# Behind the scan: halves joined by a ScalarE copy and a VectorE sum, and one GpSimd sum for the mean over 192

## The chip, the cores and the metric

The kernel runs on one core of one Trainium2 chip. The metric is the device time of one launch in microseconds, for a batch of eight images. Engines are named as in the profile: PE is TensorE, DVE is VectorE, ACT is ScalarE, POOL is GpSimd (Pool in the text), SP is SyncE, which here only issues DMAs.

## The reference, cut to what matters

Each image is 96 channels of 64 x 64 pixels. Layer 0 is a visual state space block: group norm, layer norm, a projection to 192 channels, a depthwise convolution, a selective scan in four directions, the sum of the four, a layer norm over the 192 channels, a gate, a projection back to 96, and then a channel attention block. Layer 1 is linear attention and a quantised feed-forward part. The change lies where the scan's result is normalised:

```python
y = out_y[:, 0] + inv_y[:, 0] + wh_y + invwh_y          # four directions, 192 channels
y = jnp.transpose(y, (0, 2, 1)).reshape(b, H, W, D_INNER)
y = layer_norm(y, on_g, on_b)                           # mean and variance over 192
y = y * jax.nn.silu(z)
return jnp.einsum('bhwd,cd->bhwc', y, out_proj_w)
```

## The kernel before

Channels lie on partitions, the 4096 pixels of an image on the free axis. The 192 channels don't fit on 128 partitions. The first 128 are in `ya`. The last 64 (`DR`) are in `y5`, in two halves: partitions 0 to 63 hold the sum over two of the scan's directions, partitions 64 to 127 that over the other two, and the value of a channel is the sum of both halves. ACT writes the last of `y5` at the very end of the scan.

For each of the eight images, `prep_a`, `prep_b`, `scan` and `post` run one after the other, each as a block of its own with its own instruction list per engine; an engine starts a block when all have left the one before. Semaphores order the engines within a block.

`post` (line 1345) works in eight chunks j of 512 pixels (`CH`). The order of the work on each engine is written out with `staggered`: at step t an engine does the stages with the largest lag first, each for chunk t minus its lag. The stages that matter here are those of the layer norm over 192:

- PE, lag 0, `fold(j)` (L1383 to L1387): a product of `fold_w` (which adds partition p and p + 64) with `y5` gives the 64 joined channels in the PSUM bank `yr`; two products with `ones_di` (1/192 everywhere), of `ya` and of `y5`, add up to the mean in the bank `on_mean`. Behind them comes `var_192(j - 1)` (L1396), the mean of the squares of the chunk before, which waits for Pool (`sq_added`).
- ACT, lag 1, `ln_root` (L517, L519): Ln and Exp make the inverse deviation of chunk t - 1. Then, lag 0, `yr_copy` (L1544) copies the joined channels from PSUM to `yrc`, and `on_square` (L1548, L1549) squares both centred parts once DVE has centred them.
- DVE, lag 0, `on_center` (L1662, L1664): subtracts the mean from `ya` and, once the copy is there, from `yrc`. Ahead of it in a step DVE has, from the larger lags, `ln_unit` (L524), `skip2` (L1694), `ln_center` (L507), `skip` (L1688), `on_unit` (L1669, L1671) and `gate` (L1680, L1683).
- Pool (L1641): adds the squares of the 64 channels into those of the first 64 partitions, `sqa`. Behind the eighth it clears two rows of `cpad` (L1644, L1645), and PE's first convolution product `cab1(0)` (L1415), at step 8, waits for that.

Other products of PE in a step: `out_proj` (L1402, L1403), and the sums over 96 channels for the next layer norm (L502). An f32 product of 128 x 512 shows as two instructions in the trace, so a row with x2 is one product of the code.

SP issues the DMAs that bring the gates back at the start of the block, and then clears the semaphores of the stages before. DVE waits for them in `gate(0)` and `gate(2)`.

Of the kernel before, what the change touches and what calls it, by code (L numbers as in the profile page):

```python
# [17 lines left out]
F32 = mybir.dt.float32  # L18
# [3 lines left out]
ALU = mybir.AluOpType  # L22
# [7 lines left out]
DR = DI - DA  # L30
# [15 lines left out]
NCH = L // CH  # L46
# [67 lines left out]
def build(nc, x, weights, phase_weights, setup_weights, out, gate_dram, gn_dram):  # L114
# [8 lines left out]
    def put(name, shape, dt):  # L123

        size = int(np.prod(shape[1:])) * (4 if dt == F32 else 2 if dt in (BF16, F16) else 1)
        t = nc.alloc_sbuf_tensor_at(name, shape, dt, offset=place[0])
        place[0] += (size + 31) // 32 * 32
        return t
# [7 lines left out]
    fold_w = put("fold_w", [128, 128], F32)  # L136
# [16 lines left out]
    KB16 = L * 4  # L153
# [4 lines left out]
    def big(name, slot, parts=128):  # L158
        return at(name, [parts, L], F32, slot)
# [73 lines left out]
    yrc = big("yrc", 5 * KB16, DR)  # L233
    sqa = big("sqa", KB16)
# [40 lines left out]
    with ExitStack() as ctx:  # L275
# [11 lines left out]
        post_names = """x_nat_in x_tok_in gn_stats gn_dve mean_mm gn_mm gn_act scales_ready back_first back_in yr_mm  # L287
        yr_copied on_mean_mm on_centered on_squared on_var_mm on_log on_rsqrt on_unit sq_added gated
# [88 lines left out]
        with nc.Block() as block:  # L377
# [22 lines left out]
            def _(dve):  # L400
# [6 lines left out]
                low, up = col("ident")[:, 0:DR], col("ident")[:, DR:128]  # L407
                nc.vector.tensor_tensor(fold_w[:, 0:DR], low, up, ALU.add)
                nc.vector.tensor_tensor(fold_w[:, DR:128], low, up, ALU.add)

# [60 lines left out]
        def sl(j):  # L471

            return slice(j * CH, (j + 1) * CH)
# [871 lines left out]
        def post(img, b):  # L1345
            bank = dict(zip(("yr0", "on_mean0", "on_var", "out", "ln2_mean", "ln2_var", "yr1", "on_mean1"),
# [5 lines left out]
            with nc.Block() as block:  # L1352
# [25 lines left out]
                def _(pe):  # L1378

                    def fold(j):  # L1380

                        wait_free(pe, S["on_centered"], j, 2)
                        pe.matmul(bank[f"yr{j % 2}"], fold_w[:, :], y5[:, sl(j)], start=True, stop=True)\  # L1383
                          .then_inc(S["yr_mm"], 1)
                        mean = bank[f"on_mean{j % 2}"]
                        pe.matmul(mean, col("ones_di"), ya[:, sl(j)], start=True, stop=False)
                        pe.matmul(mean, col("ones_di"), y5[:, sl(j)], start=False, stop=True)\  # L1387
                          .then_inc(S["on_mean_mm"], 1)
                        if j > 0:
                            var_192(j - 1)  # L1390
# [94 lines left out]
                    staggered((0, fold), (1, lambda j: var_192(j) if j == NCH - 1 else None), (3, out_proj),  # L1485
# [53 lines left out]
                def _(act):  # L1539
                    ln_exp_tables(act)  # L1540

                    def yr_copy(j):
                        act.wait_ge(S["yr_mm"], j + 1)
                        act.copy(yrc[:, sl(j)], bank[f"yr{j % 2}"][0:DR, :]).then_inc(S["yr_copied"], 1)  # L1544
# [92 lines left out]
                def _(pool):  # L1637

                    for j in range(NCH):
                        pool.wait_ge(S["on_squared"], j + 1)  # L1640
                        pool.tensor_tensor(sqa[0:DR, sl(j)], sqa[0:DR, sl(j)], sqr[:, sl(j)], ALU.add)\  # L1641
                            .then_inc(S["sq_added"], 1)
# [16 lines left out]
                def _(dve):  # L1659
                    def on_center(j):  # L1660
                        dve.wait_ge(S["on_mean_mm"], j + 1)
                        dve.tensor_tensor(ya[:, sl(j)], ya[:, sl(j)], bank[f"on_mean{j % 2}"], ALU.subtract)  # L1662
                        dve.wait_ge(S["yr_copied"], j + 1)
                        dve.tensor_tensor(yrc[:, sl(j)], yrc[:, sl(j)], bank[f"on_mean{j % 2}"][0:DR, :], ALU.subtract)\  # L1664
                           .then_inc(S["on_centered"], 1)
# [267 lines left out]
```

## Time and profile before

| | |
|---|---|
| median of 3 runs | 12109.58 us (12099.88 to 12118.07) |
| the profiled execution, whole time | 12101.1 us |
| its span on the core | 12099.2 us |
| PE busy | 10610.6 us, 88% |
| DVE busy | 10566.9 us, 87% |
| ACT busy | 9359.5 us, 77% |
| POOL busy | 9502.9 us, 79% |
| mean granted PE clock | 0.967 |

The rows of the timeline give the start in us from the span's start, the time in us from start to end (of a merged group of x n instructions, from the first's start to the last's end), engine, line, operation, output and inputs, and in brackets how long the engine idled before it and what it waited for. The ends of PE's instructions are modelled and overlap the next start, and DVE's and ACT's next instruction starts a little before the end of the one before it, so the distance of two starts is the better measure of what an instruction costs.

### The profile page before, as it was taken

The numbers are of one execution on the slowest core, as the hardware profiler recorded it, in microseconds if no ns is written. First come the engines' busy times: TensorE is split into PE (matmuls) and PEld (weight loads), VectorE is DVE, ScalarE is ACT, GpSimd is POOL, SyncE is SP. The second block draws the span as 40 slices with busy tenths as digits, with TensorE's granted clock in tenths as the row PEclk, the third lists the DMA queues.
The fourth block names the chain that finished last, engine by engine and source line by source line (L and its number), as shares of the span: only waits on it lengthen the run. The fifth ranks groups of instructions, "written<-read, shape, count | busy, mean of one in ns | idle before, by whom it ended". The sixth has DMA issues, their size and how long they took to land. (4 is left out here: it accounts for less than half of the span.)

```text
span 12099.2 us, 124903 instructions
## 1 busy us (share of the span) xinstructions
PE 10610.6 (88%) x35606; PEld 4918.4 (41%) x35606; DVE 10566.9 (87%) x7439; ACT 9359.5 (77%) x20340; POOL 9502.9 (79%) x4213
## 2 busy tenths in 40 slices
PE   7988889898898988989889898898988988889888
PEld 3444334443344433444334443344433444334443
DVE  6999779996799977999679996799967999689996
ACT  5888678885788867888578885788867888678885
POOL 4999459994599945999459994599945999369993
PEclk9999989999999999999999999999998999999999
DMA  4687447774477744777447774477744777447773
GB/s 136 225 225 223 116 129 225 224 220 112 132 225 223 222 108 140 223 223 221 104 143 222 223 223 99 145 224 221 222 100 144 226 225 219 98 151 224 225 222 90
DMA packets 678831, 2207.14 MB, mean 182 GB/s; under 512 B 165153, under 2 KB 167201, under 8 KB 666721
## 3 DMA queue, kind: packets, MB, share of 16 engines
q1 hardware_dynamic: 678144, 2199.17, 62.8%
q8 instruction: 287, 4.70, 0.2%
q14 instruction: 400, 3.27, 0.1%
HBM read 2101.48 MB, written 67.44 MB: 179 GB/s over the span
## 5 line engine op out<-in xcount | busy, mean ns | idle before, releaser
L1339 POOL TENSOR_TENSOR state<-state,c_sb 128x1024 f32<-128x1024 f32 x3072 | 7175.5, 2369 | 230.2 <-DMA c_sb<-bc 127.7
L1089 PE MATMUL ps<-state,wt 128*128 128x512 f32 x12288 | 5736.9, 600 | 67.1 <-ACT ya L1160 26.1
L1307 DVE TENSOR_TENSOR_SCAN state<-decay,carry,ps 128x1024 f32<-128x1024 f32 x1728 | 3988.0, 2338 | 40.7 <-issue 5.7
L1089 PEld LDWEIGHTS ps<-state,wt 128*128 128x128 f32 x12288 | 2262.9, 191 | 2256.8 <-issue 1931.2
L1213 ACT ACTIVATE dbu_t<-du_t,b_t 128x128 f32<-128x128 f32 (+1 forms) x10176 | 2951.1, 366 | 25.3 <-PE ps L1080 25.3
L1232 ACT ACTIVATE decay<-delta,a_neg 128x1024 f32<-128x1024 f32 x2304 | 2641.0, 1146 | 0.1
L1328 POOL TENSOR_TENSOR dbu<-b_sb,du 128x1024 f32<-128x1024 f32 x768 | 1814.2, 2362 | 175.2 <-DVE du L1312 152.8
L1294 DVE TENSOR_TENSOR ps<-ps,du 128x1024 f32<-128x1024 f32 x1288 | 1555.1, 1207 | 40.0 <-PE ps L1034 40.0
L1167 ACT COPY carry<-state 128x1 f32<-128x1 f32 x3072 | 568.5, 185 | 1273.4 <-DVE state L1307 1258.4
L1034 PE MATMUL ps<-parts,sel 114*128 114x512 bf16 (+1 forms) x2576 | 793.1, 390 | 794.7 <-DVE state L1307 792.9
L1307 DVE TENSOR_TENSOR_SCAN state<-ps,carry,dbu 128x1024 f32<-128x1024 f32 x576 | 1347.9, 2340 | 130.2 <-POOL dbu L1328 108.1
L1307 DVE TENSOR_TENSOR_SCAN state<-decay,ps 128x1024 f32<-128x1024 f32 x576 | 1296.2, 2278 | 13.8 <-PE ps L1080 2.2
L1080 PE MATMUL ps<-wt,dbu_t 128*128 128x128 f32 x8128 | 1098.0, 279 | 157.6 <-DVE state L1307 156.7
L1080 PEld LDWEIGHTS ps<-wt,dbu_t 128*128 128x128 f32 x8128 | 942.5, 143 | 649.6 <-DVE state L1307 329.4
L1232 ACT ACTIVATE ps<-delta,a_neg 128x1024 f32<-128x1024 f32 x768 | 853.0, 1111 | 0.0
L1034 PEld LDWEIGHTS ps<-parts,sel 114*128 114x128 bf16 (+1 forms) x2576 | 170.1, 97 | 1632.2 <-DVE state L1307 1497.2
L1655 POOL CAST h<-h16b 128x1536 fp8e5<-128x1536 f16 x64 | 116.1, 1815 | 890.5 <-DVE h16b L1780 890.5
L313 ACT ACT_TABLE_LOAD x409 | 524.7, 1283 | 73.7 <-DMA x_tok<-x 26.9
L1307 DVE TENSOR_TENSOR_SCAN state<-ps,dbu 128x1024 f32<-128x1024 f32 x192 | 437.4, 2278 | 55.7 <-POOL dbu L1328 54.8
L517 ACT ACTIVATE rs<-ps,wt 96x512 f32<-96x512 f32 (+1 forms) x320 | 218.7, 683 | 306.2 <-PE ps L502 166.5
L1641 POOL TENSOR_TENSOR sqa<-sqa,sqr 64x512 f32<-64x512 f32 x64 | 100.9, 1577 | 396.2 <-ACT sqr L1549 396.2
L1046 PE MATMUL ps<-parts,dt_w 114*128 114x512 bf16 (+1 forms) x1536 | 376.8, 389 | 30.0 <-PEq L675 30.0
(218 smaller groups left out, 10031.8 us busy)
## 6 DMA issues: line engine op xcount, KB each, us to landing
c_sb<-bc SPq DMA_DIRECT2D x2048, 512.0 KB, 4.6
c_sb<-bc SPq DMA_DIRECT2D x2048, 256.0 KB, 5.9
b_sb<-bc SPq DMA_DIRECT2D x512, 512.0 KB, 4.0
b_sb<-bc SPq DMA_DIRECT2D x512, 256.0 KB, 4.0
x_nat<-x SPq DMA_DIRECT2D x17, 1536.0 KB, 14.6
gates<-gate_a SPq DMA_DIRECT2D x8, 2048.0 KB, 6.8
x_tok<-x SPq DMA_DIRECT2D x288, 48.0 KB, 1.9
gn<-gn_t SPq DMA_DIRECT2D x8, 1536.0 KB, 7.1
```

The source lines that it names most:

```text
L313: act.add_instruction(mybir.InstLoadActFuncSet(name=nc.get_next_instruction_name(), act_func_set_id=which, ins=[], outs=[]))
L1034: mm = pe.matmul(bank[:, q * CH:(q + 1) * CH], sel[own, n, first:first + 128], part_cols(at, 2 * (T // 3), q, own), start=True, stop=True)
L1046: mm = pe.matmul(pc[:, q * CH:(q + 1) * CH], dt_w[own, p, w, :], part_cols(at, k, q, own), start=(i == 0 and p == 0), stop=(i == len(ways) ...
L1080: mm = pe.transpose(pb[n % 2][:, j * 128:(j + 1) * 128], src[:, j, :], col("ident"))
L1089: mm = pe.matmul(py[:, q * CH:(q + 1) * CH], col("ident"), state[:, slot(g, n), q * CH:(q + 1) * CH], start=(n == 0), stop=False)
L1167: act.copy(carry[:, n:n + 1], state[:, slot(g, n), last:last + 1]).then_inc(S["carried"], 1)
L1213: last = act.activation(dbu_t[turn % TRING][:, j, part], du_t[:, j, part], ACT.Copy, scale=b_t[:, g % 2, j, i:i + 1])
L1232: act.activation(pb[n % 2][:, :] if made(g, n) == BY_POOL else decay[:, n % 2, :], delta[:, g % 2, :], ACT.Exp, scale=a_neg[:, T, n:n + 1] ...
L1294: dve.tensor_tensor(pb[n % 2][:, :], pb[n % 2][:, :], du[:, g % 2, :], ALU.mult)\
L1307: dve.tensor_tensor_scan(state[:, slot(g, n), way], rate, what, 0.0 if fresh else carry[:, n:n + 1], ALU.mult, ALU.add)\
L1328: pool.tensor_tensor(dbu[:, :], b_sb[:, :], du[:, g % 2, :], ALU.mult)\
L1339: pool.tensor_tensor(state[:, slot(g, n), :], state[:, slot(g, n), :], c_sb[:, n % CRING, :], ALU.mult).then_inc(S["weighted"], 1)
```

## The change

The fold on PE goes. Instead ACT copies the upper half of `y5` down to partitions 0 to 63 of `yrc` (SBUF to SBUF, with no wait), and DVE adds the lower half to it, in `on_center`, ahead of both subtractions. A new semaphore `yr_summed` orders that sum before the subtraction from `yrc`. For the mean, Pool adds `ya` and `y5` to a new tensor `y_all` (128 x 512 per chunk, in the place of `sqa`, which is written later), and PE makes the mean with one product of it. Pool makes the sums of chunks 0 and 1 first, and that of chunk j + 2 ahead of its wait for the squares of chunk j. The constant `fold_w` and the two additions of the setup that made it go.

```diff
--- before.py
+++ after.py
@@ -133,7 +133,6 @@
     sel = put("sel", [XR3, NS, 2 * 128], BF16)
     dt_w = put("dt_w", [XR3, 3, 8, 128], BF16)
     a_neg = put("a_neg", [128, 6, NS], F32)
-    fold_w = put("fold_w", [128, 128], F32)
     d_sum = put("d_sum", [128, 2], F32)
     w1_q = put("w1_q", [C, HID], F8)
     w2_q = put("w2_q", [128, MT, C], F8)
@@ -231,6 +230,7 @@
     dbu_t = (dbu_t0, dbu_t1)
 
     yrc = big("yrc", 5 * KB16, DR)
+    y_all = big("y_all", KB16)
     sqa = big("sqa", KB16)
     sqr = big("sqr", 2 * KB16, DR)
     rs = big("rs", 3 * KB16)
@@ -284,8 +284,8 @@
         ur_in xp_mm xp_hi xp_out xp_rest xp_mid xp_low parts_zero bc_stored parts_in pre_mm delta_made delta_ready du_ready b_mm decayed dbu_ready
         dbu_pooled scanned carried weighted summed y_summed y_taken c_in_0 c_in_1 c_in_2 c_in_3 b_in_0
         bt_mm bt_out dut_mm dut_out dbut_made turned""".split()
-        post_names = """x_nat_in x_tok_in gn_stats gn_dve mean_mm gn_mm gn_act scales_ready back_first back_in yr_mm
-        yr_copied on_mean_mm on_centered on_squared on_var_mm on_log on_rsqrt on_unit sq_added gated
+        post_names = """x_nat_in x_tok_in gn_stats gn_dve mean_mm gn_mm gn_act scales_ready back_first back_in y_joined
+        yr_summed yr_copied on_mean_mm on_centered on_squared on_var_mm on_log on_rsqrt on_unit sq_added gated
         out_mm x1_ready ln2_mean_mm ln2_centered ln2_squared ln2_var_mm ln2_log ln2_rsqrt ln2_unit
         cpad_zero ln2_ready hs_zero cab1_mm sides_out side_mm gelu_out cab2_mm cb_out pooled
         pool_mm pool_mean ca1_mm ca1_out ca2_mm ca_ready x_back x1_skipped x2_ready t1_mean_mm t1_centered t1_squared
@@ -404,10 +404,6 @@
                 group_shift(dve)
 
                 nc.vector.tensor_copy(conv_w[:, :], scol(setup, "conv_w"))
-                low, up = col("ident")[:, 0:DR], col("ident")[:, DR:128]
-                nc.vector.tensor_tensor(fold_w[:, 0:DR], low, up, ALU.add)
-                nc.vector.tensor_tensor(fold_w[:, DR:128], low, up, ALU.add)
-
                 for half in range(2):
                     nc.vector.tensor_copy(sel[:, :, half * 128:half * 128 + 128],
                                           scol(setup, "sel", XR3)[:, half, :].unsqueeze(2).broadcast_to([XR3, NS, 128]))
@@ -1343,7 +1339,7 @@
 
 
         def post(img, b):
-            bank = dict(zip(("yr0", "on_mean0", "on_var", "out", "ln2_mean", "ln2_var", "yr1", "on_mean1"),
+            bank = dict(zip(("spare0", "on_mean0", "on_var", "out", "ln2_mean", "ln2_var", "spare1", "on_mean1"),
                             sum(ps, [])))
             bank.update(cab1_0=ps[3][0], cab1_1=ps[3][1])
             bank.update(zip(("sum0", "sum1", "cab2_0", "cab2_1", "ca1", "ca2"), sum(ps, [])))
@@ -1377,14 +1373,11 @@
                 @block.tensor
                 def _(pe):
 
-                    def fold(j):
+                    def mean_192(j):
 
                         wait_free(pe, S["on_centered"], j, 2)
-                        pe.matmul(bank[f"yr{j % 2}"], fold_w[:, :], y5[:, sl(j)], start=True, stop=True)\
-                          .then_inc(S["yr_mm"], 1)
-                        mean = bank[f"on_mean{j % 2}"]
-                        pe.matmul(mean, col("ones_di"), ya[:, sl(j)], start=True, stop=False)
-                        pe.matmul(mean, col("ones_di"), y5[:, sl(j)], start=False, stop=True)\
+                        pe.wait_ge(S["y_joined"], j + 1)
+                        pe.matmul(bank[f"on_mean{j % 2}"], col("ones_di"), y_all[:, sl(j)], start=True, stop=True)\
                           .then_inc(S["on_mean_mm"], 1)
                         if j > 0:
                             var_192(j - 1)
@@ -1482,7 +1475,7 @@
                         if j == NCH - 1:
                             mm.then_inc(S["kvt_mm"], 1)
 
-                    staggered((0, fold), (1, lambda j: var_192(j) if j == NCH - 1 else None), (3, out_proj),
+                    staggered((0, mean_192), (1, lambda j: var_192(j) if j == NCH - 1 else None), (3, out_proj),
                               (4, lambda j: ln_sum(pe, j, x1, S["x1_ready"], bank["ln2_mean"], S["ln2_centered"],
                                                    S["ln2_mean_mm"])),
                               (5, lambda j: ln_sum(pe, j, sq2, S["ln2_squared"], bank["ln2_var"], S["ln2_log"],
@@ -1540,8 +1533,7 @@
                     ln_exp_tables(act)
 
                     def yr_copy(j):
-                        act.wait_ge(S["yr_mm"], j + 1)
-                        act.copy(yrc[:, sl(j)], bank[f"yr{j % 2}"][0:DR, :]).then_inc(S["yr_copied"], 1)
+                        act.copy(yrc[:, sl(j)], y5[DR:128, sl(j)]).then_inc(S["yr_copied"], 1)
 
                     def on_square(j):
                         act.wait_ge(S["on_centered"], j + 1)
@@ -1636,7 +1628,15 @@
                 @block.gpsimd
                 def _(pool):
 
+                    def join(j):
+
+                        pool.tensor_tensor(y_all[:, sl(j)], ya[:, sl(j)], y5[:, sl(j)], ALU.add).then_inc(S["y_joined"], 1)
+
+                    join(0)
+                    join(1)
                     for j in range(NCH):
+                        if j + 2 < NCH:
+                            join(j + 2)
                         pool.wait_ge(S["on_squared"], j + 1)
                         pool.tensor_tensor(sqa[0:DR, sl(j)], sqa[0:DR, sl(j)], sqr[:, sl(j)], ALU.add)\
                             .then_inc(S["sq_added"], 1)
@@ -1658,9 +1658,11 @@
                 @block.vector
                 def _(dve):
                     def on_center(j):
+                        dve.wait_ge(S["yr_copied"], j + 1)
+                        dve.tensor_tensor(yrc[:, sl(j)], yrc[:, sl(j)], y5[0:DR, sl(j)], ALU.add).then_inc(S["yr_summed"], 1)
                         dve.wait_ge(S["on_mean_mm"], j + 1)
                         dve.tensor_tensor(ya[:, sl(j)], ya[:, sl(j)], bank[f"on_mean{j % 2}"], ALU.subtract)
-                        dve.wait_ge(S["yr_copied"], j + 1)
+                        dve.wait_ge(S["yr_summed"], j + 1)
                         dve.tensor_tensor(yrc[:, sl(j)], yrc[:, sl(j)], bank[f"on_mean{j % 2}"][0:DR, :], ALU.subtract)\
                            .then_inc(S["on_centered"], 1)
```

## Rows read from the trace of the kernel before

**Rows 1.** The page: its first line, and Pool's costliest group (busy, mean ns of one | idle).
```profile
span 12099.2 us, 124903 instructions
...
L1339 POOL TENSOR_TENSOR state<-state,c_sb 128x1024 f32<-128x1024 f32 x3072 | 7175.5, 2369 | 230.2 <-DMA c_sb<-bc 127.7
```

**Rows 2.** Timeline of the first image: start and end of the opening of `post`.
```profile
1338.97 1.10 PE L1383 MATMUL ps<-y,fold_w 128*128 128x512 f32 x2 [2.37 <-PEq L976]
...
1342.43 0.67 DVE L1664 TENSOR_TENSOR yrc<-yrc,ps 64x512 f32<-64x512 f32 x1
...
1393.77 5.26 PE L1415 MATMUL ps<-cpad,post_w 96*96 96x512 f32 x6 [5.36 <-POOL cpad L1645]
```

**Rows 3.** Timeline, first image: one early pass, from Pool's addition to the next.
```profile
1357.49 1.25 POOL L1641 TENSOR_TENSOR sqa<-sqa,sqr 64x512 f32<-64x512 f32 x1 [5.01 <-ACT sqr L1549]
...
1358.79 1.13 PE L1396 MATMUL ps<-sqa,wt 128*128 128x512 f32 x2 [0.48 <-POOL sqa L1641]
...
1359.96 0.69 ACT L517 ACTIVATE rs<-ps,wt 128x512 f32<-128x512 f32 x1 [2.55 <-PE ps L1396]
...
1360.68 0.63 ACT L519 ACTIVATE rs<-rs 128x512 f32<-128x512 f32 x1
...
1361.21 0.56 ACT L1544 COPY yrc<-ps 64x512 f32<-64x512 f32 x1
...
1361.81 0.68 DVE L1664 TENSOR_TENSOR yrc<-yrc,ps 64x512 f32<-64x512 f32 x1 [0.60 <-ACT yrc L1544]
...
1362.52 0.63 ACT L1548 ACTIVATE sqa<-ya 128x512 f32<-128x512 f32 x1 [0.75 <-DVE yrc L1664]
...
1363.06 0.61 ACT L1549 ACTIVATE sqr<-yrc 64x512 f32<-64x512 f32 x1
...
1363.75 1.78 POOL L1641 TENSOR_TENSOR sqa<-sqa,sqr 64x512 f32<-64x512 f32 x1 [5.01 <-ACT sqr L1549]
```

**Rows 4.** Timeline, first image: the last pass, DVE's rows and two of PE's.
```profile
1383.07 0.68 DVE L1664 TENSOR_TENSOR yrc<-yrc,ps 64x512 f32<-64x512 f32 x1 [0.47 <-ACT yrc L1544]
1383.67 0.68 DVE L524 TENSOR_TENSOR cen<-cen,rs 96x512 f32<-96x512 f32 x1
...
1384.27 0.74 DVE L1694 SCALAR_TENSOR_TENSOR x<-x,wt,x_nat 96x512 f32<-96x512 f32 x1
...
1385.68 1.02 PE L1386 MATMUL ps<-ya,wt 128*128 128x512 f32 x2
1386.19 1.06 DVE L1669 SCALAR_TENSOR_TENSOR ya<-ya,wt,rs 128x512 f32<-128x512 f32 x1
...
1386.53 1.02 PE L1387 MATMUL ps<-y,wt 128*128 128x512 f32 x2
...
1388.50 0.74 DVE L1683 SCALAR_TENSOR_TENSOR yrc<-yrc,wt,gate_r 64x512 f32<-64x512 f32 x1
1389.16 0.67 DVE L1662 TENSOR_TENSOR ya<-ya,ps 128x512 f32<-128x512 f32 x1
...
1390.30 0.68 DVE L1664 TENSOR_TENSOR yrc<-yrc,ps 64x512 f32<-64x512 f32 x1 [0.47 <-ACT yrc L1544]
```

**Rows 5.** By line (ns min/median/max of all), and one held-up row of the timeline.
```profile
L1641 POOL TENSOR_TENSOR sqa<-sqa,sqr x64: 1254/1697/1849, 1344.4 to 11936.1; 64x512 f32<-64x512 f32 x64
...
L1662 DVE TENSOR_TENSOR ya<-ya,ps x64: 669/671/689, 1341.8 to 11933.1; 128x512 f32<-128x512 f32 x64
...
1357.47 1.81 DVE L1671 SCALAR_TENSOR_TENSOR yrc<-yrc,wt,rs 64x512 f32<-64x512 f32 x1
```

**Rows 6.** Busy by stretch (PE, PEld, DVE, ACT, POOL, clock, DMA); second image's timeline.
```profile
1392.00:1397.00 5.00, 3.23 (x4) 1.25 (x5) 0.25 (x1) 0.87 (x2) 1.43 (x3) 0.50 0.00 0
...
2846.73 1.10 PE L1383 MATMUL ps<-y,fold_w 128*128 128x512 f32 x2 [2.37 <-PEq L976]
...
2860.29 2.08 PE L1396 MATMUL ps<-sqa,wt 128*128 128x512 f32 x2 [3.15 <-POOL sqa L1641]
...
2905.45 5.40 PE L1415 MATMUL ps<-cpad,post_w 96*96 96x512 f32 x6 [5.36 <-POOL cpad L1645]
```

## The prediction

> **What bounds the kernel now.** The change touches only the opening of the stage behind the scan, once per image, so I read the span [rows 1], then the timeline of that opening for the first image, then the same stretch of the others. In it PE starts its first fold at 1338.97 us and the stretch is over when PE starts the first convolution product (L1415) at 1393.77 us: 54.80 us [rows 2]. Between them DVE runs eight passes; the last instruction of on_center (L1664) starts first at 1342.43 and last at 1390.30, so the seven steps from pass to pass take 47.87 us together [rows 2, 4]. L1415 waits for Pool's memsets behind its eighth addition to sqa (L1641), so whatever lengthens a pass arrives at L1415 one to one.
>
> What sets a pass is a ring of waits, seen whole in the timeline from 1357.49 to 1363.75 us [rows 3]: Pool adds sqr into sqa, PE makes the variance, ACT does Ln and Exp, and only behind them in ACT's order the copy of yr for the next pass; DVE subtracts the mean from it (L1664), ACT squares twice, Pool adds again. The reader is to see that each starts as its forerunner ends: 6.26 us from one Pool start to the next, the shortest pass there is. In the late passes DVE is nearly full as well. From L1664 at 1383.07 to L1664 at 1390.30 are 7.23 us, and DVE works without a gap from 1383.07 until L1662 starts at 1389.16, 6.09 us; only behind L1662 (0.67 us) are there 0.47 us of idleness [rows 4]. PE issues eight f32 products per pass there, 0.85 us from one start to the next (L1386 at 1385.68, L1387 at 1386.53), some 6.9 us in all [rows 4]. So three things lie close together: ring, DVE, PE.
>
> **The change, part by part.** *PE* loses two of its three f32 products per pass (the fold and one of the two of the mean), 1.72 us per pass. They lie beside the ring: before, they delayed the variance behind Pool's end by some 0.7 us in the late passes, which is the difference of 7.23 against 6.26 plus what Pool was held up. That is the whole gain.
>
> *ACT's copy* reads y5 in SBUF, not PSUM. The copy takes 0.56 us, an ACT pass over 64x512 from SBUF takes 0.61 us (L1549) [rows 3]; no trace shows the copy itself from SBUF, so 0 to 0.1 us, and I take 0.04 per pass. It no longer waits for PE, but it stays behind Ln and Exp of the pass before in ACT's order, so it comes no earlier.
>
> *DVE* gets a sum of 64x512, queued behind that copy and ahead of both subtractions. Now L1662 runs before the copy arrives and only L1664 is on the ring. After the change both the sum and L1662 stand between the copy and L1664. A DVE tensor_tensor of this size occupies DVE some 0.61 us (L1662 and L1664 show 0.67 to 0.68 us from start to end, and the next starts 0.06 to 0.07 before that end) [rows 3 to 5]. Two of them: 1.22 us more on the ring in each of seven steps. With two SBUF inputs the sum could cost up to 0.74, what the scalar_tensor_tensor group takes; from below 0.55; I take 0.61, as L524, also of two SBUF inputs, is issued in 0.60.
>
> *Pool* gets eight joins of 128x512. The nearest rows are its own sum of 64x512 at 1.25 us (L1641, shortest) and the scan's product of 128x1024 at 2.37 us, half of which is 1.18 [rows 1, 5]; I take 1.25. Pool has the time: it idles 5.0 us before each addition [rows 3]. Joins 0 and 1 come first; join j+3 is issued right behind the addition for j, so y_all is there two passes before PE wants it, and the only wait on it that counts is at j = 0. What costs is DVE. When Pool adds while DVE works on SBUF alone, one holds up the other: L1671 at 1357.47 took 1.81 us in place of 0.74, as L1641 had begun at 1357.49 (1.07 us lost) and Pool's additions range from 1.25 to 1.85 us, median 1.70 [rows 3, 5]. L1662, with one input in PSUM, was never stretched in 64 times (0.669 to 0.689) [rows 5]. Each join is issued exactly when DVE stands in its four SBUF-only instructions on_unit and gate, so I charge one more stall of 1.07 us of DVE per pass, between 0 and 1.25.
>
> Here a rule of the Trainium skill speaks against the change: "SBUF — State Buffer", section Who interferes with whom, says that a DVE instruction with two SBUF inputs contends with a GpSimd instruction that reads SBUF, and that the later one fully blocks. By that the join would cost a whole 1.25 us of DVE, and a late pass would come out near 8.6 in place of 8.5; the trace shows 1.07 for a full collision and less for others.
>
> *The sum.* Ring: 6.26 + 1.22 + 0.04 = 7.52 us. DVE in a late pass: 6.09 us up to L1662 [rows 4], which holds one stall of 0.33 (L1669 at 1.06 in place of 0.74), plus sum, L1662 and its share 2 x 0.61, plus the join's stall 1.07 to 1.25: 8.4 to 8.6 us. The seven steps: pass 1: 7.52. Pass 2: Pool held up by 0.60 as now (1.85 against 1.25), 8.12. Pass 3: 7.52. Pass 4: ring with Pool at its median 1.70, 7.96. Passes 5 to 7: DVE, 8.5 each. Together 56.6 us against 47.87: +8.75. At the start: join 0 and join 1 from 1338.97, 2.5 us, hold the SBUF-only sum until 1341.5; sum and L1662 end near 1342.65, so L1664 starts 0.2 us later than 1342.43. An undisturbed opening goes from 54.80 to 63.75 us.
>
> **The clock** comes on top. Behind a pause of PE of 5.36 us, which ended at 1393.77, the granted clock was 0.50 from 1392 to 1397 [rows 2, 6], the lower of the two levels (1.2 of 2.4 GHz). A cold variance product takes 2.08 us (at 2860.29) in place of 1.12 to 1.13 [rows 3, 6]: 0.95 more on the ring. The second image fell to it with today's work already, in a pause of 3.15 us: from L1383 at 2846.73 to L1415 at 2905.45 are 58.72 us, 3.92 over the first image [rows 6]. Over the eight images such losses make about 12 us now (450.3 against 8 x 54.80, by the same two rows of each image, of which those of the first two stand). Afterwards PE has two products, 1.7 us, per 7.5 us in passes 1 to 3, with pauses over 5 us, so I count every variance of these passes cold: 3 x 0.95 = 2.85. For passes 4 to 7 and the first mean I add 1.15, since DVE hides most of it: 4.0 per image. The bounds are 0 and 9 (seven passes cold, the start, and a refill of about 1.5). "TensorE: Matmul & The Clock Gate" (What's actually happening) of the Trainium skill calls the throttled state the default that activity releases; that too speaks against taking products from PE, and the second image agrees with it.
>
> Total: 8 x (63.75 + 4.0) = 542.0 against 450.3: +92 us. All else is nothing: two setup additions of 64 columns once, 512 bytes of SBUF, a semaphore more to clear on SP while the stage before waits for other things; behind L1415 the order is unchanged and everything shifts. Transfers for gate have more room, not less. On the profiled execution (12101.1 us, span 12099.2) this gives 12193; the median of the runs is 12109.58, 8.5 above it, so I forecast 12202 us.
>
> **Rivals.** *Stalls and clock stay small* (20%). Joins fall into gaps of DVE and PE stays warm: all late passes at the ring's 7.96, seven steps 55.0, opening 54.80 + 7.1 + 0.2 = 62.1; 8 x 62.1 = 497 against 450.3: +47 us, 12156. For it: the ring's length needs no assumption. Against: DVE had only 0.47 us to spare [rows 4].
> *Clock collapses* (15%): the 9 us of the upper bound, 8 x 72.75 = 582: +132 us, 12241. For it: the second image; against: six products per late pass refill it.
> *PE was the bound* (4%), the other side: if the eight products per pass decided the late passes and the sum hid in DVE's 0.47 us of idleness, three passes would lose 1.72 us each and the 12 us of cold clock would be mostly saved: -8 x 5.2 - 12 = -53 us, 12057. It decides only if the copy arrives over 1.2 us earlier than now, ahead of Ln and Exp; by rows 3 the copy stands behind both.
> *It does not do what it says* (5%): the work is meant to come off PE, but all that comes is an exchange, two DVE instructions on the ring against PE's delay, Pool's hold-ups and today's cold clock. With Pool never held up, seven steps of 7.52 are 52.6 us, 4.8 over now, less the 1.5 us of cold clock per image: 8 x 3.3 = +26 us, 12136, the edge of what can be measured, and within it if the sum's sources cost less than 0.61. Against: Pool's median of 1.70 [rows 5].
>
> **How the numbers follow.** The forecast case has 56%, the two rivals beside it 20 and 15, the last two 4 and 5. The range takes in the two neighbours and the bounds of stall and clock: 12150 to 12250. A measurement of this kernel tells 0.2%, 24 us, from no change. Faster by more: 0.04. Within: 0.05. Slower by more: 0.91.
>
> **What would show it.** Right: L1664's successor starts 7.5 us apart in early and about 8.5 in late passes; the copy starts right behind Exp as now, then three DVE instructions in a row; on_unit or gate of 1.8 us twice per pass; variance products of 2 us in passes 1 to 3; the first L1415 some 68 us behind the stage's first instruction. Wrong: steps of 7.2 or less, an idle DVE in late passes, joins over 2 us, or a stretch behind L1415 that changes length.

## The result and the profile after

The changed kernel takes 12163.44 us (median) against 12109.58: a ratio of 1.0043, 95% interval 1.0031 to 1.0055, so 38 to 67 us slower. Beside three experiments the same kernel came to 12165.9 against 12107.6, a ratio of 1.0049 (1.0037 to 1.0062). The forecast was 12202, +92 us, with a range from 12150 to 12250: the sign and the place were right, the size was too large by some 38 us (34 by the second comparison). One run of number 10 below took 36467 us at a granted clock of 0.37 and is left out of its figures; every other run was undisturbed.

The head of the page after, engines with busy time and share:

```profile
span 12161.6 us, 124573 instructions
...
PE 10554.1 (87%) x35350; PEld 4874.2 (40%) x35350; DVE 10616.7 (87%) x7501; ACT 9369.2 (77%) x20340; POOL 9588.1 (79%) x4277
```

PE lost 56.5 us of work, DVE got 49.8 more, Pool 85.2 more. The page alone can't say what that costs, as no engine is full. The opening of the stage can. I call **opening** the time from SP's first DMA of a gate, which is the start of the block, to the first product of `cab1`, and **step** the distance between two starts of the last instruction of `on_center` (L1664 before, L1666 after). Means of the eight images of one execution, worked out from the timelines:

| kernel | first | steps 1 to 7 | eight openings |
|---|---|---|---|
| before | 3.91 | 6.26, 7.21, 6.99, 6.79, 7.24, 7.23, 7.24 | 450.7 |
| after | 3.82 | 8.28, 9.17, 8.63, 8.42, 8.02, 7.64, 7.85 | 522.4 |
| after, second execution | 3.92 | 8.23, 9.17, 9.41, 8.11, 8.10, 7.65, 7.83 | 527.1 |

The openings are 72 to 76 us longer. The span outside them is 11648.5 us before, 11639.2 and 11640.5 after; over all 14 profiles of this study it lies between 11621.7 and 11654.9 (the numbers stand below).

Timeline of the changed kernel, first image, one undisturbed late step; it answers to [rows 3]:

```profile
1391.80 1.26 POOL L1641 TENSOR_TENSOR sqa<-sqa,sqr 64x512 f32<-64x512 f32 x1 [4.93 <-ACT sqr L1541]
...
1393.12 1.13 PE L1389 MATMUL ps<-sqa,wt 128*128 128x512 f32 x2 [1.14 <-POOL sqa L1641]
...
1394.28 0.69 ACT L513 ACTIVATE rs<-ps,wt 128x512 f32<-128x512 f32 x1
...
1395.00 0.63 ACT L515 ACTIVATE rs<-rs 128x512 f32<-128x512 f32 x1
...
1395.65 0.62 ACT L1536 COPY yrc<-y 64x512 f32<-64x512 f32 x1
...
1396.30 0.68 DVE L1662 TENSOR_TENSOR yrc<-yrc,y 64x512 f32<-64x512 f32 x1 [0.60 <-ACT yrc L1536]
1396.91 0.67 DVE L1664 TENSOR_TENSOR ya<-ya,ps 128x512 f32<-128x512 f32 x1
...
1397.51 0.67 DVE L1666 TENSOR_TENSOR yrc<-yrc,ps 64x512 f32<-64x512 f32 x1
...
1398.21 0.63 ACT L1540 ACTIVATE sqa<-ya 128x512 f32<-128x512 f32 x1 [1.95 <-DVE yrc L1666]
...
1399.44 1.27 POOL L1641 TENSOR_TENSOR sqa<-sqa,sqr 64x512 f32<-64x512 f32 x1 [6.38 <-ACT sqr L1541]
```

The reader is to see the same ring as in [rows 3], two members longer: Pool to Pool is 7.64 us instead of 6.26. From the copy's start to the last subtraction's start are 1.86 us (1395.65 to 1397.51), where they were 0.60 (1361.21 to 1361.81); the copy itself starts 0.65 behind Exp's start instead of 0.53. Together that is the 1.38. DVE had 0.60 us of idleness ahead of the sum: in this step it isn't full, and the ring sets it.

The second cost is in the early steps. Two of PE's rows, the second variance of the image and the product behind it:

```profile
1359.82 2.07 PE L1389 MATMUL ps<-sqa,wt 128*128 128x512 f32 x2 [5.39 <-POOL sqa L1641]
1361.69 1.91 PE L1395 MATMUL ps<-ya,wt 128*96 128x512 f32 x2
```

The variance took 2.07 us behind a pause of 5.39, the time of the lower clock level. In the eight images 18 of the first 24 variances took over 1.4 us, in the second execution 21, and before 3.

The third is DVE against Pool. The fifth step of the first image:

```profile
1383.83 1.37 POOL L1641 TENSOR_TENSOR sqa<-sqa,sqr 64x512 f32<-64x512 f32 x1 [4.71 <-ACT sqr L1541]
...
1384.41 1.33 DVE L1671 SCALAR_TENSOR_TENSOR ya<-ya,wt,rs 128x512 f32<-128x512 f32 x1
...
1385.16 1.71 POOL L1633 TENSOR_TENSOR y_all<-ya,y 128x512 f32<-128x512 f32 x1
...
1385.67 1.75 DVE L1673 SCALAR_TENSOR_TENSOR yrc<-yrc,wt,rs 64x512 f32<-64x512 f32 x1
...
1387.79 0.62 ACT L1536 COPY yrc<-y 64x512 f32<-64x512 f32 x1
1388.01 0.73 DVE L1685 SCALAR_TENSOR_TENSOR yrc<-yrc,wt,gate_r 64x512 f32<-64x512 f32 x1
1388.67 0.67 DVE L1662 TENSOR_TENSOR yrc<-yrc,y 64x512 f32<-64x512 f32 x1
```

Two of DVE's four SBUF-only instructions are stretched, one by Pool's addition and one by its join (1.33 and 1.75 in place of 0.74). The copy is done at 1388.41, the sum starts at 1388.67, when DVE comes free: here the stalls cost a quarter of a microsecond. A collision can also lengthen Pool's own addition, and that one stands on the ring: the second addition of an image takes 1.85 us instead of 1.25, in both kernels.

### The profile page after: what moved, and what is told of

Read it like the earlier page. It is cut to its first block and busy times, and to the rows that moved or that the text cites. A ratio compares the mean times of both kernels' runs of the same rounds, so it can differ in the third digit from the quotient of the medians.

```text
span 12161.6 us, 124573 instructions
## 1 busy us (share of the span) xinstructions
PE 10554.1 (87%) x35350; PEld 4874.2 (40%) x35350; DVE 10616.7 (87%) x7501; ACT 9369.2 (77%) x20340; POOL 9588.1 (79%) x4277
## 5 line engine op out<-in xcount | busy, mean ns | idle before, releaser
L1641 POOL TENSOR_TENSOR sqa<-sqa,sqr 64x512 f32<-64x512 f32 x64 | 93.8, 1465 | 329.2 <-ACT sqr L1541 329.2
```

## The experiments

Three theories were tried against each other: **ring** (two DVE instructions behind a copy that stands behind Ln and Exp), **stall** (Pool's joins hold up DVE), **clock** (PE falls to its lower level in the early steps). All ratios are against the kernel before, with runs on the same chip. A variance product is called cold if it took over 1.4 us. The kernels with an opening for each:

| kernel | first | steps 1 to 7 | eight openings | ratio (95%) |
|---|---|---|---|---|
| 1 no joins | 3.66 | 7.75, 9.17, 8.65, 8.43, 7.76, 7.64, 7.65 | 513.4 | 1.0041 (1.0028 to 1.0055) |
| 2 joins only | 3.60 | 6.38, 7.61, 7.49, 7.43, 7.64, 6.65, 6.70 | 455.8 | 0.9992 (0.9984 to 1.0001) |
| 3 PE's products kept | 4.52 | 7.63, 9.08, 8.72, 8.16, 7.98, 7.95, 7.65 | 521.3 | 1.0048 (1.0035 to 1.0061) |
| 4 ya first | 4.60 | 7.91, 8.69, 7.78, 7.86, 8.03, 7.21, 7.16 | 501.7 | 1.0034 (1.0021 to 1.0046) |
| 5 copy early | 3.96 | 1.80, 10.48, 8.08, 7.77, 8.18, 7.02, 7.88 | 469.1 | 1.0008 (0.9999 to 1.0017) |
| 6 copy early, no joins | 3.47 | 1.91, 9.21, 7.63, 6.71, 7.37, 6.96, 6.97 | 429.6 | 0.9978 (0.9968 to 0.9988) |
| 7 PE warm | 3.96 | 7.80, 8.43, 8.38, 8.07, 8.27, 7.67, 7.88 | 511.4 | 1.0043 (1.0030 to 1.0056) |
| 8 before, copy first | 4.32 | 2.61, 7.45, 7.27, 6.54, 7.62, 6.90, 6.87 | 425.8 | 0.9976 (0.9966 to 0.9987) |
| 8 again | 4.52 | 2.62, 7.44, 7.46, 6.60, 6.99, 7.08, 7.13 | 428.2 | 0.9973 (0.9964 to 0.9982) |
| 9 joins, copy first | 3.83 | 2.37, 7.80, 8.23, 7.62, 7.65, 6.64, 6.71 | 434.4 | 0.9981 (0.9972 to 0.9990) |
| 10 late joins, copy first | 4.15 | 2.58, 7.48, 7.32, 6.53, 6.93, 6.59, 6.62 | 413.3 | 0.9965 (0.9951 to 0.9978) |

**1. One half alone: copy and sum, no joins.**

```diff
-                        pe.wait_ge(S["y_joined"], j + 1)
-                        pe.matmul(bank[f"on_mean{j % 2}"], col("ones_di"), y_all[:, sl(j)], start=True, stop=True)\
+                        pe.matmul(mean, col("ones_di"), ya[:, sl(j)], start=True, stop=False)
+                        pe.matmul(mean, col("ones_di"), y5[:, sl(j)], start=False, stop=True)\
```

> The changed kernel without Pool's sums: ACT's copy and DVE's sum stay, PE makes the mean from two products (of ya and of y5) as before, and no y_all is made. Ring theory (the two DVE instructions between the copy and the last subtraction are the price): steps of 7.6 to 8.1 us between the last subtractions of a chunk, seven steps about 56 us against 47.87, 45 to 65 us slower than before, as slow as the change. Stall theory (what Pool's sums take from DVE is the price): steps as before, within 20 us of before. Clock theory (PE has too little work in the early steps): between them, since PE has three products per step here against two in the change and five before: some 10 us faster than the change.

12154.2 us against 12107.6, within the ring's range. Steps 6 and 7 stand at 7.64 and 7.65, which is to a hundredth what the changed kernel takes where nothing disturbs it (step 6 always, step 7 in six of eight images; its mean of 7.85 comes from two with a cold seventh variance), though Pool makes no join and PE has one product more. So the ring's 1.38 us is the copy's and the sum's, not the joins'. The openings are 9 to 14 us shorter than the change's, but that isn't the joins' price alone: with its extra product this kernel has 10 cold variances among the first 24 where the change has 18 and 21, and the first step, cold in five images of the change and in one here, gives 4 of the 9 us by itself. The clock theory's "some 10 us faster" fits as well. Where a join's stall shows without the clock is step 5: 7.75 instead of 7.97, about 2 us over eight images.

**2. The other half alone: joins, fold kept.**

```diff
-                        pe.matmul(mean, col("ones_di"), ya[:, sl(j)], start=True, stop=False)
-                        pe.matmul(mean, col("ones_di"), y5[:, sl(j)], start=False, stop=True)\
+                        pe.wait_ge(S["y_joined"], j + 1)
+                        pe.matmul(bank[f"on_mean{j % 2}"], col("ones_di"), y_all[:, sl(j)], start=True, stop=True)\
```

> The kernel before with only Pool's sums added and the mean made from one product; the fold on PE and ACT's copy out of PSUM stay. Ring theory: steps as before (6.26 to 7.2 us), within 15 us of before, or a little faster, as PE has one product less per step. Stall theory: 5 steps with a sum of Pool in them, up to 1.07 us each, eight times: 30 to 45 us slower.

12099.9 us, no change that can be measured, and not the 30 to 45 us slower of the stall theory; the ring theory's "steps as before" is only half true. Steps 1 to 5 hold a join. The first is hardly longer (6.38); steps 2 to 5 are 0.4 to 0.6 us longer than before, the two without a join shorter (6.65 and 6.70 against 7.23), as PE has seven products instead of eight. Not all of it is stall: step 2 is longer because its variance is cold in seven images, against three before; step 5, at 7.65 in every image, is the join's. Together the joins cost what the product gives. A late join at work, timeline of this kernel's first image:

```profile
1384.32 1.71 POOL L1641 TENSOR_TENSOR y_all<-ya,y 128x512 f32<-128x512 f32 x1
1384.40 1.12 PE L1396 MATMUL ps<-sqa,wt 128*128 128x512 f32 x2
1384.83 1.75 DVE L1679 SCALAR_TENSOR_TENSOR yrc<-yrc,wt,rs 64x512 f32<-64x512 f32 x1
...
1386.82 0.56 ACT L1544 COPY yrc<-ps 64x512 f32<-64x512 f32 x1
1387.16 0.73 DVE L1691 SCALAR_TENSOR_TENSOR yrc<-yrc,wt,gate_r 64x512 f32<-64x512 f32 x1
1387.82 0.67 DVE L1670 TENSOR_TENSOR ya<-ya,ps 128x512 f32<-128x512 f32 x1
```

The copy ends at 1387.38, while DVE is still in its gate: in this step DVE, held up once more, has become the bound (7.64).

**3. The clock, first try: PE keeps as many products, ahead of the mean.**

```diff
                         wait_free(pe, S["on_centered"], j, 2)
+                        for _ in range(2):
+                            pe.matmul(bank[f"spare{j % 2}"], col("ones_di"), y5[:, sl(j)], start=True, stop=True)
```

> The changed kernel with two products of y5 into a bank that nobody reads, ahead of the product for the mean, so that PE has as many products per step as before. Clock theory: variance products of 1.12 us instead of 2.07 in the early steps; seven steps about 55 us against 57 to 59, 20 to 26 us faster than the change, so 25 to 35 us slower than before. Rival (PE's products cost time by themselves, as they lie ahead of the variance in PE's order): as slow as the change or slower.

12167.4 us, as slow as the change. The clock theory's 20 to 26 us didn't come. All eight first and third variances were warm, but the second was still cold in all images (1.6 to 2.1 us): in all 8 cold ones of the first 24, against 18 and 21. Step 1 falls to 7.63 by it, but the products ahead of the first mean made that one late (first: 4.52 instead of 3.8 to 3.9), and step 3 (8.72) gains 0.7 us on the change's second execution but nothing on the first. There Pool's third addition collides with DVE in six of eight images, here in the first:

```profile
1367.42 2.51 POOL L1643 TENSOR_TENSOR sqa<-sqa,sqr 64x512 f32<-64x512 f32 x1 [5.35 <-ACT sqr L1543]
1368.07 0.74 DVE L1684 SCALAR_TENSOR_TENSOR ya<-ya,wt,gate_a 128x512 f32<-128x512 f32 x1
1368.73 1.74 DVE L1687 SCALAR_TENSOR_TENSOR yrc<-yrc,wt,gate_r 64x512 f32<-64x512 f32 x1
```

It takes 2.51 us instead of 1.25, and the step 8.89 with a warm variance, where the change has steps of 8.58 with a cold one and a short addition. In the change's two executions the same addition took 2.5 us in three and in seven images; this collision weighs as much in step 3 as the clock, and no run separates the two. So I tried again as number 7.

**4. A smaller dose: the subtraction from ya ahead of the copy's wait.**

```diff
+                        dve.wait_ge(S["on_mean_mm"], j + 1)
+                        dve.tensor_tensor(ya[:, sl(j)], ya[:, sl(j)], bank[f"on_mean{j % 2}"], ALU.subtract)
                         dve.wait_ge(S["yr_copied"], j + 1)
                         dve.tensor_tensor(yrc[:, sl(j)], yrc[:, sl(j)], y5[0:DR, sl(j)], ALU.add).then_inc(S["yr_summed"], 1)
-                        dve.wait_ge(S["on_mean_mm"], j + 1)
-                        dve.tensor_tensor(ya[:, sl(j)], ya[:, sl(j)], bank[f"on_mean{j % 2}"], ALU.subtract)
```

> The changed kernel with the subtraction from ya ahead of the wait for the copy and of the sum, so that one DVE instruction less stands behind the copy. Ring theory: every step 0.61 us shorter (7.03 where it was 7.64), 8 x 7 x 0.61 = 34 us faster than the change, about 22 us slower than before. Rival (DVE is simply full, its order is no matter): as slow as the change, 55 us slower than before.

The ratio fell from 1.0049 to 1.0034, some 18 us, where 34 were expected; the openings fell by 21 to 25 us. The late step is 7.16 instead of 7.64, 0.48 less and not 0.61:

```profile
1396.96 0.62 ACT L1536 COPY yrc<-y 64x512 f32<-64x512 f32 x1
...
1397.60 0.68 DVE L1664 TENSOR_TENSOR yrc<-yrc,y 64x512 f32<-64x512 f32 x1
...
1398.32 0.68 DVE L1666 TENSOR_TENSOR yrc<-yrc,ps 64x512 f32<-64x512 f32 x1
```

The subtraction now starts 0.72 us behind the sum, since it needs the sum's end; with another instruction between them they stood 0.61 apart each. And the first subtraction waits for the mean (first: 4.60). The direction is the ring's: one member less, a shorter step, the fifth excepted (8.03), where DVE's stalls decide.

**5. The ring opened: the copies two chunks ahead.**

```diff
-                    staggered((0, yr_copy), (0, on_square),
+                    yr_copy(0)
+                    yr_copy(1)
+                    staggered((0, on_square), (0, lambda j: yr_copy(j + 2) if j + 2 < NCH else None),
```

> The changed kernel with ACT's copies two chunks ahead (they wait for nothing), so that they no longer stand behind Ln and Exp. Ring theory: the ring is then Pool's addition, the variance, Ln, Exp and the two squares, about 5.0 us, and DVE sets the late steps, 7.3 to 8.3 us with the stalls; openings of about 55 us, 60 to 80 us faster than the change, 0 to 20 us faster than before. Stall or clock theory: the change's price stays, 30 us or more slower than before.

12110.2 us against 12101.9, ratio 1.0008: all but a sixth of the distance to the kernel before is gone by the place of the copies, with every copy, sum and join still there. The openings fall from some 525 to 469.1 us. So most of the 54 us wasn't what DVE and ACT have more to do, but where on the ring they do it. That isn't yet a like for like comparison, as the kernel before gains 27 to 30 us by the same move (number 8): with the copy off the ring in both, the change still costs 1.0008 against 0.9976, some 39 us. Number 6 shows where these are. The gain expected on top (60 to 80 us faster than the change, some 50 were measured) didn't come: seven steps take 51.2 us in the mean where the kernel before takes 48.95. Step 1 is now 1.80 (the second centring waits for nothing) and step 2 takes it back, 10.48. And the clock still costs: step 7, which holds no join, takes 6.97 us in three images and 8.26 to 10.11 in four. The longest, in the third image, with a granted clock of 0.50 from 4404 to 4410:

```profile
4408.34 2.02 PE L1396 MATMUL ps<-yrc,wt 64*96 64x512 f32 x2
...
4410.40 0.74 DVE L1692 SCALAR_TENSOR_TENSOR x<-gn,wt,ps 96x512 f32<-96x512 f32 x1 [2.97 <-PE ps L1396]
```

Here DVE waits 2.97 us for PE's out_proj.

**6. The same without joins, where DVE is the bound.**

```diff
-                    join(0)
-                    join(1)
                     for j in range(NCH):
-                        if j + 2 < NCH:
-                            join(j + 2)
```

> The changed kernel with the copies two chunks ahead and without Pool's sums (PE makes the mean from two products). With the copy off the ring, DVE sets the late steps, so a stall of DVE must show here if anywhere. Stall theory: the steps with a sum of Pool in them (7.7 to 8.3 us in the run with the copies ahead and Pool's sums) fall by up to 1.07 us to about 7.0, some 25 to 35 us faster over eight images. Rival (the stalls are free there too): as fast as with Pool's sums.

12072.4 us against 12102.0, 38 us below number 5, and the openings 39.5 us shorter: more than the 25 to 35 expected. The timelines show it in one step. With the joins (number 5), first image:

```profile
1375.36 1.88 POOL L1635 TENSOR_TENSOR y_all<-ya,y 128x512 f32<-128x512 f32 x1
...
1376.04 1.75 DVE L1675 SCALAR_TENSOR_TENSOR yrc<-yrc,wt,rs 64x512 f32<-64x512 f32 x1
...
1377.72 0.73 DVE L1684 SCALAR_TENSOR_TENSOR ya<-ya,wt,gate_a 128x512 f32<-128x512 f32 x1
```

and without them (number 6) the step has one stretched instruction, that of Pool's addition, and the next come at 0.66 us:

```profile
1376.40 1.74 DVE L1670 SCALAR_TENSOR_TENSOR ya<-ya,wt,rs 128x512 f32<-128x512 f32 x1
1378.06 0.73 DVE L1672 SCALAR_TENSOR_TENSOR yrc<-yrc,wt,rs 64x512 f32<-64x512 f32 x1
1378.72 0.73 DVE L1681 SCALAR_TENSOR_TENSOR ya<-ya,wt,gate_a 128x512 f32<-128x512 f32 x1
```

Step 4 falls from 7.77 to 6.71, by 1.06, which is the full collision of [rows 5]. So a join costs a microsecond where DVE binds and, by step 5 of number 1, a quarter or so where the ring does. But this kernel differs from number 5 by a product more on PE as well, and of the 39.5 us not all is stall: steps 3 to 5 give 18.6, step 2 10, the first mean, which waits for a join in number 5, 4, and step 7, without a join, 7 by the clock (10 cold variances of 64 here, 22 there). Note that this kernel, which has the copy and the sum that made the change slow, beats the kernel before by 30 us and is level with number 8, which has the fold (0.9978 against 0.9976): off the ring, copy and sum cost no more than the fold that they replace. That is the test of the ring theory.

**7. The clock, second try: products that nobody reads in PE's pauses.**

```diff
                         if j > 0:
                             var_192(j - 1)
+                        if j < 4:
+                            for _ in range((2, 4, 4, 2)[j]):
+                                pe.matmul(bank["spare1"], col("ones_di"), y5[:, sl(NCH - 1)], start=True, stop=True)
```

> The changed kernel with 2, 4, 4 and 2 products of y5 into a bank that nobody reads, behind the variance in the first four steps, where PE would be idle. Clock theory: the variances of the first three steps take 1.12 us instead of 2.07, each step 0.95 us less; 20 to 30 us faster than the change, 25 to 35 us slower than before. Rival (the cold variance is hidden): no faster than the change.

```profile
1356.91 1.13 PE L1392 MATMUL ps<-sqa,wt 128*128 128x512 f32 x2 [2.81 <-POOL sqa L1644]
1357.88 3.60 PE L1386 MATMUL ps<-y,wt 128*128 128x512 f32 x8
```

The second variance takes 1.13 us; in all only 2 of the first 24 took over 1.4. The second step falls from 9.17 to 8.23 in six of eight images, 0.94 as expected. The openings are 11 to 16 us shorter than the change's, and the ratio 1.0043 against 1.0049, some 7 us: the time misses the expected 20 to 30. Steps 5 and 7 still have cold variances, and step 3 takes 7.92 in four images and up to 9.28 in the others. The two ratios' intervals overlap widely, so it is the rows, not the time, that bear out that the lower clock is on the ring; how much of the time it costs they don't settle.

**8. The kernel before, with its copy ahead of Ln and Exp.**

```diff
+                    def copy_then_root(j):
+                        if j + 1 < NCH:
+                            yr_copy(j + 1)
+                        ln_root(act, j, bank["on_var"], S["on_var_mm"], rs, S["on_log"], S["on_rsqrt"], 128)
```

> The kernel before with ACT's copy of the next chunk ahead of Ln and Exp of this one. Ring theory: the first steps fall from 6.26 towards 5.0 us; the late ones stay near PE's 6.9 (eight products); 20 to 40 us faster than before. Rival (PE's eight products set all steps): within 10 us of before.

12074.7 and, in a second set of runs, 12071.9 us: 27 and 30 us faster than before. The same move that mends the change also helps the old kernel, whose ring had the same member. The first three steps average 5.8 us (2.6, 7.45 and 7.3) instead of 6.8. The late steps stay near 7.2 in many images:

```profile
1381.00 1.12 PE L1383 MATMUL ps<-y,fold_w 128*128 128x512 f32 x2
1381.11 0.74 DVE L1692 SCALAR_TENSOR_TENSOR x<-gn,wt,ps 96x512 f32<-96x512 f32 x1 [0.79 <-PE ps L1403]
...
1381.96 1.02 PE L1386 MATMUL ps<-ya,wt 128*128 128x512 f32 x2
...
1382.82 1.02 PE L1387 MATMUL ps<-y,wt 128*128 128x512 f32 x2
...
1383.68 1.02 PE L1396 MATMUL ps<-sqa,wt 128*128 128x512 f32 x2
```

PE goes from product to product, and DVE waits for PE's out_proj (0.79): with the ring out of the way, PE's eight products are the bound. Numbers 9 and 10 test that by taking one away.

> The kernel before with ACT's copy ahead of Ln and Exp once more, as the measure beside the run with late sums: 20 to 35 us faster than before.

**9 and 10. Fewer products for PE, with joins that stall DVE and with joins that don't.** Number 9 is number 2 with the move of number 8. Number 10 has joins for the last four chunks only, all made at the very start:

```diff
+                    for j in range(NCH // 2, NCH):
+                        pool.tensor_tensor(y_all[:, sl(j)], ya[:, sl(j)], y5[:, sl(j)], ALU.add).then_inc(S["y_joined"], 1)
                     for j in range(NCH):
                         pool.wait_ge(S["on_squared"], j + 1)
```

> The same on the kernel with Pool's sums and the mean from one product (fold on PE kept): PE has seven products per step, DVE up to 1.07 us of stall more in five steps. If PE set the late steps of the run before this one, this is 10 to 20 us faster than it, but for the stalls; if DVE sets them, it is 10 to 20 us slower.

> The kernel before with ACT's copy ahead of Ln and Exp, and with Pool's sums for the last four chunks alone, made at the very start, where DVE has nothing that they could stall. PE has seven products in the late steps. Expected: the late steps fall from 7.2 to about 6.7 us, 8 to 15 us faster than without these sums, 35 to 40 us faster than before. Rival: the late steps are set by DVE; then no gain over the copy alone.

Number 9: 12081.3 us, a little behind number 8 (ratio 0.9981 against 0.9976, not told apart by the times); its steps show both sides: 7.62 and 7.65 with a join, 6.64 and 6.71 without. Number 10: 12058.4 against 12102.0, ratio 0.9965, with number 8 at 0.9973 beside it: 10 us or so less, as expected, but the intervals overlap. Its openings of 413.3 us are the shortest of all, and its late steps 6.59 to 6.93 where number 8 has 6.99 to 7.13 (6.87 to 7.62 in its first execution). By the openings, then, a join is worth having for PE's sake where nothing on DVE stands beside it, with the fold left on PE; the times alone don't prove it.

**What stays open.** The openings of the change are 72 to 76 us longer, the times 54 and 58 us, 18 us less in both comparisons. About half of that is which executions were profiled: that of the kernel before (12101.1) lies 8.5 and 6.5 us under the two medians of its runs, those of the change lie at the median and 3.5 us over, so the profiled executions themselves differ by 62 and 68 us. The other 8 to 9 us lie outside the openings. The spans without the openings are, in the order of the table: 11621.7, 11651.3, 11654.0, 11648.4, 11635.3, 11641.2, 11632.8, 11641.7, 11654.9, 11653.1 and 11637.5. The six profiles of kernels with the fold (before, 2, 8 twice, 9, 10) average 11647.8, the eight with copy and sum 11639.1. The difference of 8.7 us has the size of that other half, but it is small against the scatter within either group (17 and 32 us from lowest to highest), and no profile shows a stage that it comes from. I leave it as not settled.

## Why the prediction was right, and where its size was off

**The ring.** Right, and it carried the sign. Expected 7.52 us for an undisturbed step, measured 7.64. From the copy's start to the last subtraction's the sum holds, 1.26 us more as counted; the 0.12 is a term put at nothing, as the copy starts 0.65 behind Exp's start, which had been 0.53. Number 1 shows that copy and sum make this alone, number 4 that one member less shortens it, and number 6 beside number 8 that off the ring the two cost nothing that can be measured.

**The late steps** failed: 8.5 us each for steps 5 to 7, measured 8.02, 7.64 and 7.85 (7.65 where the clock isn't low). The failing step is the sum "DVE in a late pass", and it has two slips that the profile of before could have told. First, it charged a join to every late step, though its own part on Pool says that join j+3 stands behind the addition for j; with eight chunks the last is behind the fifth addition, so the sixth and the seventh step have none, and there the ring's 7.64 holds. Secondly it took 6.09 us for DVE from a step with `ln_unit` in it, which the fifth has not (0.6 us). 8.5 less 0.6 is 7.9, and 8.02 was measured there. Together about 2 us per image, 16 us over eight images: nearly half of what the forecast is too high by.

**The stall's own price** was right as a size (1.07, and number 6 shows 1.06 in step 4) and wrong as a term: where the ring sets the step, DVE has slack that swallows most of it. In the changed kernel the stall shows in step 5 alone, about 2 us of 522; of the 9 to 14 us between it and number 1 the larger part is the clock's. Once the ring is open, leaving the joins out (with a product more on PE) gives 38 us.

**The clock.** 4.0 us per image were added. With all variances warm the opening would be about 62.0 us (3.6, then 7.63, 8.22, 7.64, 8.16, 7.97, 7.64, 7.64, and 3.5 to the end), and 65.3 were measured, so 3.3. The place was right: 2.07 us in steps 1 to 3. The size came out near, but that is partly luck: the 62.0 supposes that nothing else moves when the products are warm, and Pool's third addition, 2.51 us long in six images of number 3 and 1.25 in the others, shows that more varies in these steps than the clock. Number 7 got back 11 to 16 of these 26 us of openings, number 3 at most 6. So that the clock's price is 26 us is worked out, not shown. No run shows the "refill of about 1.5" in the upper bound.

**The start**: 0.2 us was said. On average it came out at the same as before (3.82 against 3.91), as in two of the eight images before the first took over 5 us and in none of the change's; undisturbed it is 3.58 to 4.07 instead of 3.50. The mechanism was another than forecast: Pool makes three joins first and not two, and the sum doesn't wait for them (1.11 us beside them in the first image); the first subtraction then waits for the mean.

**The rest of the gap**: openings of 522 to 527 instead of 542 explain 15 to 20 us of the 34 to 38, and the missing 18 are the point above: half of it the choice of the executions, half not explained. That the measured time lies inside the range thus owes something to width; its lower part was put there for "stalls and clock stay small".

**The rivals.** The measured time is nearest to the price of "stalls and clock stay small" (+47), but for another reason: the clock didn't stay small, the stalls were hidden, and 18 us of the openings' growth don't show in the times. "Clock collapses" is out: late variances are cold in 4 and 2 of 40 cases. "PE was the bound" is false for the change and true behind it: in number 8, with the ring open, PE is what binds. "It does not do what it says" was right that the change is an exchange (PE lost 56.5 us of work, and no step became shorter), and too low in price (+26): it took Pool's additions as never held up and today's cold clock as gone, and the second addition still took 1.85 us and the clock cost more. The joins are early: PE waited for one only at the start of each image, for the first two products of the mean.

## What to carry to other kernels

Before an engine's work is handed to another, find the ring of waits that sets the step, and ask whether the new instructions stand on it or beside it: here one more sum on DVE behind ACT's copy cost most of 54 us on it, and next to nothing when that copy was issued two chunks earlier (number 6 against number 8). What the ring had hidden comes due when it is opened: Pool's sums then cost up to a microsecond per step. So compare both kernels with the ring opened before judging the change. An in-order engine can put an instruction that waits for nothing (the copy) behind one that waits for the slowest engine; such an instruction belongs as far ahead as its buffers allow. Count from the loop how many steps really hold a term before it is multiplied by all of them.

## What the runs showed of the hardware

- Two dependent DVE instructions of 64x512, the second reading what the first wrote, start 0.72 us apart; with an independent one between, 0.61 each (number 4 against the change). I had counted 0.61 for both.
- ACT's copy of 64x512 out of SBUF takes 0.616 to 0.617 us in all 64 cases of the changed kernel, out of PSUM 0.562 to 0.581 in the kernel before.
- Pool's sum of two SBUF tensors takes as long for 64 partitions as for 128: 1.254 us at least for L1641 [rows 5], 1.252 for the join at its shortest. Beside DVE's SBUF-only instructions the addition goes up to 2.51 and the join up to 1.92 in the changed kernel, and DVE's from 0.73 to as much as 1.88.
- Ahead of the second variance PE pauses 5.39 us or more in all eight images of the changed kernel, and the variance then runs at the lower clock level in all eight. In the kernel before the same pause is 3.15 us in every image, and three of eight variances are at the lower level; in number 7 it is 2.81, with products ahead of it, and two are. So a pause of the same length was followed by either level.
